# The reciprocal root of a per-row norm: ScalarE's square root against a guess on the bits and three Newton steps on VectorE

## The chip, the cores and the metric

The kernel runs on one core of one Trainium2 chip. The metric is device microseconds of one execution. Five engines work beside each other and meet at semaphores: TensorE (PE; PEld is its weight load), VectorE (DVE), ScalarE (ACT), GpSimd (POOL), which here issues indirect DMAs, and SyncE (SP), which issues plain ones.

## The reference

A graph layer with a GRU cell, then a layer of eight experts, on 6250 rows of 256 values and 200000 edges sorted by their target:

```python
def _layernorm(x, axis=-1, eps=1e-05):
    m = jnp.mean(x, axis=axis, keepdims=True)
    v = jnp.var(x, axis=axis, keepdims=True)
    return (x - m) / jnp.sqrt(v + eps)
...
        msg = h[edge_src] + relvectors[edge_rel]
        red = jax.ops.segment_sum(msg, edge_dst, num_segments=h.shape[0])
        return _gru_cell(red, h, w_ih, w_hh, b_ih, b_hh)
...
        gate_scores = x @ Wg + bg
        _, idx = jax.lax.top_k(gate_scores, K)
...
    x = x + _L0_gnn_ref(_layernorm(x, axis=-1), L0_gnn_relvectors, L0_gnn_w_ih, L0_gnn_w_hh, L0_gnn_b_ih, L0_gnn_b_hh, src, dst, edge_type_16)
    x = x + _L0_ffn_ref(_layernorm(x, axis=-1)[None], L0_ffn_Wg, L0_ffn_bg, L0_ffn_W1, L0_ffn_b1, L0_ffn_W2, L0_ffn_b2)[0]
```

The change concerns the second `_layernorm`, on the rows that the graph layer has left, ahead of the experts.

## The kernel before

The work has four parts. A prologue normalizes `x` (the first norm, in seven chunks, with its own square roots at line 789), writes the result as `h_table` to DRAM and lays out the edges. Then come half steps, numbered h = 0, 1, 2 and on, in which three things run interleaved. (1) The *head*, the first 230 rows of 512 edges: VectorE builds one-hot matrices (`head_build`, tiles `lone`, `cone`, with `wone` and `tone` per pair of rows), PE multiplies them into counts in bursts (`head_burst`, L1704 and L1709), ScalarE copies each burst's counts out of PSUM into `amat` (`move_group`, L827 and L830), and PE multiplies `amat` with the node table in pieces (`head_piece`, L1722). The bursts use two PSUM banks in turn, so a burst waits until the burst ahead of it is copied. (2) The *tail*, the other 162 rows of edges: POOL gathers the source rows by indirect DMAs into `ring` (L709, eight DMAs a step, room for two steps), and PE sums them (`sums`, L1649). While there are bursts in the head, a gather also waits until PE has reached a certain burst (`gather_turns`). (3) The GRU and the choice of experts, tile by tile: 25 tiles of 250 rows, in a fixed order and mostly six half steps apart. When the tiles are done, 56 expert blocks follow (from about 1200 us on).

What each engine does in half step h is written out by hand in four functions `fast` (ScalarE L888, VectorE L1371, PE L1822, POOL L722), with `stage_of(h, n)` naming the tile that is at its stage n. Each engine works through its own list in order, so a wait stops all that is behind it. A tile's stages, with tile i six half steps behind tile i - 1:

- stage 0: PE transposes the rows of the table (`transpose_h`), ScalarE copies them (`copy_hT`, tile `h_h`);
- stage 1: PE multiplies them for the new state (`gate_hn`, L1760), at the end of its half step, when VectorE has `h_l` ready;
- stage 2: VectorE makes the low part of the rows (`low_h`, L1251, tile `h_l`), behind `add_sums`, `build` and `lay_indices`; later `fast_sums`; PE `gate_r`; ScalarE `bias_hn` and the first tanh (`gate_r`, L857);
- stages 3 to 6: the other gates; VectorE blends (`blend`), PE transposes back (`transpose_gru`, L1785), which also waits until the tile ahead has its slots;
- stage 7: VectorE adds the rows of `x` and takes mean and variance (`residual`, L1273), last but one in its half step; ScalarE takes the root (`root`, L872), ahead of that half step's bursts;
- stage 8: VectorE takes the reciprocal and writes the normed rows `xrow` (`second_norm`, L1287); PE transposes them (`transpose_x2`, L1793); POOL later scatters them to `expert_rows`;
- stages 10 to 12: scores, the two best experts (`choose`), their rows' numbers (`number`).

So stage 7 of a tile is stage 1 of the next, and stage 8 of a tile is stage 2 of the next: `residual` of a tile is followed on VectorE by `low_h` of the next one, and PE's `gate_hn` of the next tile waits for that.

ScalarE's square root and its tanh need different tables: the compiler has put a table load (ACT_TABLE_LOAD) ahead of each root and ahead of each tile's first tanh; copies and sums with a bias need none. On VectorE `link` makes every instruction wait until the one ahead has finished.

Of the kernel before, what the change touches and what calls it, by code (L numbers as in the profile page):

```python
# [11 lines left out]
I32 = mybir.dt.int32  # L12
# [3 lines left out]
ALU = mybir.AluOpType  # L16
ACT = mybir.ActivationFunctionType
# [8 lines left out]
EPS = 1e-5  # L26
UP = 2048.0
DOWN = 1.0 / UP
# [37 lines left out]
SUB = 125  # L66
# [167 lines left out]
def groups_of(h):  # L234
    return [g for g in range(len(GROUPED)) if HALF_OF[g] == h]


def bursts_of(h):

    out = []  # L240
    for g in groups_of(h):
        alone = len(BANKS[BANK_OF[g]]) == 1 and GROUPED[g][2] < GC
        before = out[-1][-1] if out else None
        if out and BANK_OF[before] == BANK_OF[g]:
            out[-1].append(g)
        elif out and alone and len(out[-1]) == 1 and len(BANKS[BANK_OF[before]]) == 1 and GROUPED[before][2] < GC:
            out[-1].append(g)
        else:
            out.append([g])
    return out  # L250
# [13 lines left out]
def stage_of(h, offset):  # L264

    return [i for i in range(TILES) if BEGIN[i] + offset == h]
# [51 lines left out]
def gnn_ffn_kernel(nc, x, src, dst, etype, rel, w_ih, w_hh, b_ih, b_hh, Wg, bg, W1, b1, W2, b2,  # L318
# [6 lines left out]
    with ExitStack() as ctx:  # L325
        def sb(name, shape, dt=F32):
            return ctx.enter_context(nc.sbuf_tensor(name, shape, dt))
# [48 lines left out]
        mv = sb("mv", [128, 2, LN_J, 2])  # L376
        var = sb("var", [128, 2, LN_J])
        std = sb("std", [128, 2, LN_J])
        rstd = sb("rstd", [128, 2, LN_J])
        nmr = sb("nmr", [128, 2, LN_J])  # L380
        idx = sb("idx", [128, IDXR, SC], I32)
        onehot = sb("onehot", [128, 2, SC, WIN], F16)
        onetype = sb("onetype", [128, 2, FULL], F16)
# [85 lines left out]
        with ExitStack() as early:  # L469
# [21 lines left out]
            a_ready a_used a_windows a_group a_moved a_cons a_high a_low a_merged a_added s_groups s_slots  # L491
            g_idx g_type g_onehot g_counts g_cts g_agg g_half g_added g_ramp
            h_loaded x_loaded x_stored h_trans hT_ready h_l_ready red_ready hn_done hn_ready r_done r_ready rhn_ready
            z_done z_ready in_done pre_n n_ready gru_ready gru_trans x1_ready var_ready std_ready x2n_ready x2_trans
            x2h_ready x2l_ready scores_done mask_ready ranks_done slots_ready
            raw_loaded w_maxed w_tops w_trans w_diag w_spread w_scales w_high w_low w_stored w_loaded
            head_free tab_ready late_loaded
# [7 lines left out]
         a_ready, a_used, a_windows, a_group, a_moved, a_cons, a_high, a_low, a_merged, a_added, s_groups, s_slots,  # L505
         g_idx, g_type, g_onehot, g_counts, g_cts, g_agg, g_half, g_added, g_ramp,
         h_loaded, x_loaded, x_stored, h_trans, hT_ready, h_l_ready, red_ready, hn_done, hn_ready, r_done, r_ready, rhn_ready,
         z_done, z_ready, in_done, pre_n, n_ready, gru_ready, gru_trans, x1_ready, var_ready, std_ready, x2n_ready, x2_trans,
         x2h_ready, x2l_ready, scores_done, mask_ready, ranks_done, slots_ready,
         raw_loaded, w_maxed, w_tops, w_trans, w_diag, w_spread, w_scales, w_high, w_low, w_stored, w_loaded,  # L510
         head_free, tab_ready, late_loaded,
# [259 lines left out]
        def _(act):  # L771
# [39 lines left out]
            def move_counts(n):  # L811
                act.wait_ge(counts_done, n + 1)
                nc.scalar.activation(cts[:, :], P[0][:, 256:256 + STEP_G * WIN], ACT.Copy).then_inc(cts_ready, 1)
# [19 lines left out]
            def high_sums(b):  # L833
                act.wait_ge(a_cons, b + 1)
                if b:
                    act.wait_ge(a_merged, b)
                used = BATCHED[b][1] * BATCHED[b][2]
                nc.scalar.activation(s_h[0:used, :], P[1 + 3 * (b % 2)][0:used, 0:D], ACT.Copy).then_inc(a_high, 1)

            def copy_hT(i):  # L840
                act.wait_ge(h_trans, i + 1)
                if i:
                    act.wait_ge(gru_ready, i)
                nc.scalar.activation(h_h[:, :, :].rearrange("p k t -> p (k t)"), P[6][:, 0:KT * T], ACT.Copy, scale=DOWN).then_inc(hT_ready, 1)

            def bias_hn(i):
                act.wait_ge(hn_done, i + 1)
                if i:
                    act.wait_ge(gru_trans, i)
                for m in range(KT):  # L850
                    ins = nc.scalar.activation(oT[:, m, :], P[7][:, m * T:(m + 1) * T], ACT.Identity, bias=bhhc[:, 4 + m:5 + m])
                ins.then_inc(hn_ready, 1)
# [16 lines left out]
                    ins = nc.scalar.activation(rT[:, m, :], oT[:, m, :], ACT.Tanh, bias=bihc[:, 4 + m:5 + m])  # L869
                ins.then_inc(n_ready, 1)  # L870

            def root(i):  # L872
                act.wait_ge(var_ready, i + 1)
                nc.scalar.activation(std[0:SUB, 0, 0:2], var[0:SUB, 0, 0:2], ACT.Sqrt, scale=DOWN * DOWN).then_inc(std_ready, 1)

            def high_x2(i):
                act.wait_ge(x2_trans, i + 1)
                nc.scalar.activation(x2h[:, :, :].rearrange("p k t -> p (k t)"), P[5][:, 0:KT * T], ACT.Copy).then_inc(x2h_ready, 1)
# [9 lines left out]
            def fast():  # L888
                act.wait_ge(s_small, 1)
                move_counts(0)  # L890
                for h in range(ENDS):
                    n, s = divmod(h, 2)
                    for i in stage_of(h, 2):
                        bias_hn(i)
                    for i in stage_of(h, 7):
                        root(i)
                    if h + 4 in ADDED_AT:
                        high_sums(ADDED_AT.index(h + 4))
                    bursts = bursts_of(h)
                    for g in bursts[0] if bursts else []:  # L900
                        move_group(g)
                    for i in stage_of(h, 0):
                        copy_hT(i)
                    for i in stage_of(h, 2):
                        gate_r(i)
                        if 1 <= i <= WJOBS:
                            high_weights(i - 1)
                    for i in stage_of(h, 4):
                        gate_z(i)
                        gate_n(i)  # L910
                    for g in groups_of(h)[len(bursts[0]):] if bursts else []:
                        move_group(g)
                    for i in stage_of(h, 8):
                        high_x2(i)
                    if s == 1 and n + 1 < NS:
                        move_counts(n + 1)

            def general():
                act.wait_ge(s_small, 1)
                for b in range(BANDS):  # L920
                    with act.Fori(0, STEPS * BW) as v:
                        act.wait_ge(g_counts, v + (b * (STEPS * BW) + 1))
                        nc.scalar.activation(cts[:, :], P[0][:, 256:256 + STEP_G * WIN], ACT.Copy).then_inc(g_cts, 1)
                    for i in range(b * BT, b * BT + BT):
                        copy_hT(i)
                        bias_hn(i)
                        gate_r(i)
                        if 1 <= i <= WJOBS:
                            high_weights(i - 1)
                        gate_n(i)  # L930
                        gate_z(i)
                        root(i)
                        high_x2(i)

            paths(act, fast, general)

            def high_rows(b):
# [29 lines left out]
        def _(dve):  # L967
            count = [0]

            def link(ins):  # L970
                count[0] += 1
                ins.then_inc(dve_chain, 1)
                dve.wait_ge(dve_chain, count[0])
# [299 lines left out]
            def residual(i):  # L1273
                dve.wait_ge(gru_trans, i + 1)
                dve.wait_ge(x_loaded, 16 * (i + 1))
                x1f = x1[:, :, :].rearrange("p j d -> p (j d)")
                nc.vector.tensor_tensor(x1f, P[5][0:SUB, :], x1f, ALU.add).then_inc(x1_ready, 1)
                dve.wait_ge(x1_ready, i + 1)
                for j in range(2):
                    ins = nc.vector.bn_stats(st[0:SUB, j, :], x1[:, j, :])  # L1280
                link(ins)
                for j in range(2):
                    ins = nc.vector.bn_aggr(mv[0:SUB, 0, j, :], st[0:SUB, j, :])
                link(ins)
                nc.vector.tensor_scalar_add(var[0:SUB, 0, 0:2], mv[0:SUB, 0, 0:2, 1], EPS).then_inc(var_ready, 1)

            def second_norm(i, t):  # L1287
                dve.wait_ge(std_ready, i + 1)
                if i >= 2:
                    dve.wait_ge(scattered[i % 2], 64 * (i // 2))  # L1290
                link(nc.vector.reciprocal(rstd[0:SUB, 0, 0:2], std[0:SUB, 0, 0:2]))
                nc.vector.tensor_scalar(xrow[:, i % 2, :, D:D + 1].bitcast(I32), tok[0:SUB, :].unsqueeze(2), float(T * t), None, ALU.add)
                for j in range(2):
                    ins = nc.vector.tensor_scalar(xrow[:, i % 2, j, 0:D], x1[:, j, :], mv[0:SUB, 0, j, 0:1], rstd[0:SUB, 0, j:j + 1],
                                                  ALU.subtract, ALU.mult)
                ins.then_inc(x2n_ready, 1)
# [691 lines left out]
```

## Time and profile before

| | |
|---|---|
| time before, median of 3 runs | 1543.21 us (1542.58 to 1543.78) |
| profiled execution, own time | 1541.31 us |
| its span | 1539.3 us |
| its mean granted clock of TensorE | 0.922 |
| share of the span: PE, DVE, ACT, POOL | 84%, 65%, 48%, 65% |
| ACT_TABLE_LOAD, ahead of L874 and of L857 | 25 and 25, 32.1 us each |

The profile is of one execution. A row of a timeline names start, duration, engine, line, operation, what is written and read, and in brackets how long the engine stood idle before and what ended that. "issue" is idle time that nothing in the profile explains. A row of the waits names who waited for whom, the sum, the number of times and the longest.

### The profile page before, as it was taken

What the parts mean: (1) busy time and instruction counts of PE and PEld (TensorE: products, weight loads), DVE (VectorE), ACT (ScalarE), POOL (GpSimd) and SP (SyncE); (2) the same over time, 40 slices, a digit from 0 to 9 for tenths busy, and PEclk for the clock granted to TensorE, in tenths of its full rate; (3) what the DMA queues carried; (4) which work ended last, traced back from release to release, by engine and by line L of the source; (5) the groups of instructions that cost most, each with busy time, mean ns of one, the idle gap of its engine ahead of it and who ended that gap; (6) DMA issues with size and microseconds to landing.
All of it is one profiled execution on the core that took longest, in us unless ns stands there. A gap on an engine that the chain in (4) does not pass through costs nothing. (4 is left out here: it accounts for less than half of the span.)

```text
span 1539.3 us, 36184 instructions
## 1 busy us (share of the span) xinstructions
PE 1289.3 (84%) x12887; PEld 1054.1 (68%) x12887; DVE 1002.2 (65%) x2768; ACT 732.5 (48%) x1489; POOL 993.8 (65%) x868
## 2 busy tenths in 40 slices
PE   1159998999999999999998989876464799999995
PEld 1135566777677777777777777765364699999995
DVE  7866765666677777777788877873355455555552
ACT  6524454554444555555444433321122576677663
POOL 2077764776667777777777777777753265555554
PEclk9659999999999999999999989987686899999998
DMA  9586622544445455454544544444762455555551
GB/s 291 177 203 185 192 82 85 144 130 111 117 124 140 140 144 145 138 148 136 137 138 138 143 128 119 112 115 123 246 181 57 101 88 91 97 90 86 91 97 25
DMA packets 131963, 201.46 MB, mean 131 GB/s; under 512 B 28356, under 2 KB 99549, under 8 KB 130631
## 3 DMA queue, kind: packets, MB, share of 16 engines
q0 software_dynamic: 60032, 110.76, 30.0%
q1 hardware_dynamic: 71751, 88.31, 19.8%
q8 instruction: 111, 1.82, 0.5%
q14 instruction: 69, 0.57, 0.1%
HBM read 152.03 MB, written 51.10 MB: 132 GB/s over the span
## 5 line engine op out<-in xcount | busy, mean ns | idle before, releaser
L709 POOL DMA_INDIRECT ring<-h_table,idx x648 | 681.9, 1052 | 293.4 <-issue 210.5
L1722 PE MATMUL P<-hs,amat 128*126 128x512 f16 (+4 forms) x1568 | 404.7, 391 | 0.0
L827 ACT ACTIVATE amat<-P 128x300 f16<-128x300 f32 (+4 forms) x440 | 175.9, 446 | 250.3 <-PE P L1709 249.0
L763 POOL DMA_INDIRECT out_dram<-yo,xrows x112 | 177.3, 1583 | 161.2 <-DVE yo L1586 106.4
L1722 PEld LDWEIGHTS P<-hs,amat 128*126 128x126 f16 (+4 forms) x1568 | 182.4, 130 | 93.3 <-issue 8.6
L1704 PE MATMUL P<-cone,lone 128*128 128x294 f16 (+4 forms) x920 | 181.5, 293 | 44.3 <-ACT amat L827 38.2
L1577 DVE SCALAR_TENSOR_TENSOR gl<-gT,scales,gh 128x512 f16<-128x512 f32 x112 | 84.9, 758 | 138.9 <-ACT gh L954 138.9
L718 POOL DMA_INDIRECT expert_rows<-xrow,slots x100 | 125.2, 1252 | 66.7 <-DVE slots L1329 36.6
L1186 DVE TENSOR_TENSOR cone<-src_t,twice 128x1176 f16<-128x1176 f16 (+4 forms) x230 | 164.4, 715 | 0.0
L1936 PE MATMUL P<-xh,w_all 128*128 128x256 f16 x896 | 157.5, 274 | 0.0
L1949 PE MATMUL P<-w_all,gh 128*128 x896 | 149.8, 273 | 0.6 <-DVE gl L1577 0.6
L1704 PEld LDWEIGHTS P<-cone,lone 128*128 128x128 f16 x920 | 80.2, 100 | 97.9 <-ACT amat L827 48.4
L950 ACT ACTIVATE gT<-P,b1cur,scales 128x256 f32<-128x256 f32 x224 | 113.3, 555 | 43.8 <-PE P L1936 43.8
L830 ACT ACTIVATE amat<-P 128x500 f16<-128x500 f32 (+1 forms) x124 | 81.0, 660 | 101.9 <-PE P L1709 98.7
L1186 DVE TENSOR_TENSOR lone<-slo,twice 128x512 f16<-128x512 f16 x230 | 96.3, 419 | 42.1 <-PE P L1704 41.6
L1936 PE MATMUL P<-xl,w_all 128*128 128x256 f16 x448 | 122.9, 274 | 0.0
L1949 PE MATMUL P<-w_all,gl 128*128 x448 | 122.1, 273 | 0.0
L1649 PE MATMUL P<-onehot,ring 128*128 128x48 f16 x2592 | 87.4, 189 | 37.4 <-DMA ring<-h_table,idx 37.4
L1649 PEld LDWEIGHTS P<-onehot,ring 128*128 128x128 f16 x2592 | 80.5, 100 | 39.0 <-DMA ring<-h_table,idx 39.0
L1756 PE MATMUL P<-h_h,whh_h 128*128 128x250 f32 x300 | 92.8, 309 | 6.3 <-DVE h_l L1251 6.3
L1151 DVE TENSOR_TENSOR acc<-P,acc 128x96 f32 x162 | 41.6, 257 | 82.5 <-PE P L1649 56.0
L1936 PEld LDWEIGHTS P<-xh,w_all 128*128 x896 | 88.2, 98 | 10.3 <-issue 0.2
(244 smaller groups left out, 2734.9 us busy)
## 6 DMA issues: line engine op xcount, KB each, us to landing
raw<-in_L_ffn_W_dram SPq DMA_DIRECT2D x32, 512.0 KB
xrows<-expert_rows SPq DMA_DIRECT2D x56, 257.0 KB, 3.1
ring<-h_table,idx POOLq DMA_INDIRECT x648
w_parts<-parts SPq DMA_DIRECT2D x16, 512.0 KB
w_all<-w_parts SPq DMA_DIRECT2D x8, 1024.0 KB
h_in<-h_table SPq DMA_DIRECT2D x25, 250.0 KB
x<-in_x_dram SPq DMA_DIRECT2D x25, 250.0 KB
out_dram<-x SPq DMA_DIRECT2D x25, 250.0 KB
```

The source lines that it names most:

```text
L709: nc.gpsimd.indirect_dma_start(out=ring[:, r, j, :], out_offset=None, in_=h_dram, in_offset=bass.IndirectOffsetOnAxis(ap=idx[:, slot, g * ...
L718: nc.gpsimd.indirect_dma_start(out=xs_dram, out_offset=bass.IndirectOffsetOnAxis(ap=slots[:, i % 2, c * 2 + j:c * 2 + j + 1], axis=0), in_ ...
L763: nc.gpsimd.indirect_dma_start(out=out, out_offset=bass.IndirectOffsetOnAxis(ap=xrows[:, b % XR, j, D:D + 1].bitcast(I32), axis=0), in_=yo ...
L827: nc.scalar.activation(amat[:, b % 2, :, s * aw:(s + 1) * aw], bank[:, 0:HIS * aw].rearrange("p (h w) -> p h w", w=aw), ACT.Copy).then_inc ...
L950: ins = nc.scalar.activation(gT[:, b % 2, s, :], P[2 + p % 3][:, (s % 2) * TB:(s % 2 + 1) * TB], ACT.Gelu, bias=b1cur[:, b % 2, s:s + 1], ...
L1186: return nc.vector.tensor_tensor(chunk_pairs(buf, row, size), of.unsqueeze(2).to_broadcast(shape), nums.unsqueeze(1).to_broadcast(shape), ...
L1649: ins = nc.tensor.matmul(to, ring[:, r * STEP_G + g, j, at:at + 128], onehot[:, k, g * GC + j, :], start=False, stop=(g == STEP_G - 1 and ...
L1704: nc.tensor.matmul(counts_of(g, aw)[:, 0:HI * aw], src_of[:, m, :, t], dst_of[:, m, :, t], start=(n == 0), stop=(n == k - 1)).then_inc(a_u ...
L1722: nc.tensor.matmul(both, amat[:, b % 2, hi, 0:used], hs[:, hi, :], start=(hi == 0), stop=False)
L1756: ins = nc.tensor.matmul(to, a[:, k, row + m * 128:row + (m + 1) * 128], b[:, k, :], start=(n == 0), stop=(n == len(ops) - 1))
L1936: ins = nc.tensor.matmul(to, weights(b, a * WCH + k * H + s * 128, 128), v[:, b % 2, k, :], start=(n == 0), stop=(n == len(ops) - 1))
L1949: ins = nc.tensor.matmul(to, a[:, b % 2, s, j * 128:(j + 1) * 128], weights(b, (2 + w) * WCH + s * D, D), start=(n == 0), stop=(n == len(o ...
```

## The change

ScalarE's `root`, its two calls and the semaphores `var_ready` and `std_ready` go. In `residual` the variance plus epsilon is also scaled by DOWN squared, where the activation's `scale` did so; then VectorE halves the bits as an integer, subtracts them from a constant (a first guess of the reciprocal root) and improves the guess in three Newton steps of three instructions. Every one of the 12 is linked to the one before. The reciprocal in `second_norm` goes, and with it its wait for the root.

```diff
@@ -378,6 +378,7 @@
         nmr = sb("nmr", [128, 2, LN_J])
+        newton = sb("newton", [128, 4, 2])
         idx = sb("idx", [128, IDXR, SC], I32)
...
@@ -869,10 +870,6 @@
-            def root(i):
-                act.wait_ge(var_ready, i + 1)
-                nc.scalar.activation(std[0:SUB, 0, 0:2], var[0:SUB, 0, 0:2], ACT.Sqrt, scale=DOWN * DOWN).then_inc(std_ready, 1)
-
             def high_x2(i):
...
@@ -892,8 +889,6 @@
                     for i in stage_of(h, 2):
                         bias_hn(i)
-                    for i in stage_of(h, 7):
-                        root(i)
                     if h + 4 in ADDED_AT:
...
@@ -1282,13 +1276,19 @@
                 for j in range(2):
                     ins = nc.vector.bn_aggr(mv[0:SUB, 0, j, :], st[0:SUB, j, :])
                 link(ins)
-                nc.vector.tensor_scalar_add(var[0:SUB, 0, 0:2], mv[0:SUB, 0, 0:2, 1], EPS).then_inc(var_ready, 1)
+                v, y, a, bits = [newton[0:SUB, n, :] for n in range(4)]
+                link(nc.vector.tensor_scalar(v, mv[0:SUB, 0, 0:2, 1], EPS, DOWN * DOWN, ALU.add, ALU.mult))
+                link(nc.vector.tensor_scalar(bits.bitcast(I32), v.bitcast(I32), 1, None, ALU.logical_shift_right))
+                link(nc.vector.tensor_scalar(y.bitcast(I32), bits.bitcast(I32), -1.0, float(0x5F3759DF), ALU.mult, ALU.add))
+                for step in range(3):
+                    link(nc.vector.tensor_tensor(a, y, v, ALU.mult))
+                    link(nc.vector.scalar_tensor_tensor(a, a, -0.5, y, ALU.mult, ALU.mult))
+                    to = y if step < 2 else rstd[0:SUB, 0, 0:2]
+                    link(nc.vector.scalar_tensor_tensor(to, a, 1.5, y, ALU.add, ALU.mult))
 
             def second_norm(i, t):
-                dve.wait_ge(std_ready, i + 1)
                 if i >= 2:
                     dve.wait_ge(scattered[i % 2], 64 * (i // 2))
-                link(nc.vector.reciprocal(rstd[0:SUB, 0, 0:2], std[0:SUB, 0, 0:2]))
                 nc.vector.tensor_scalar(xrow[:, i % 2, :, D:D + 1].bitcast(I32), tok[0:SUB, :].unsqueeze(2), float(T * t), None, ALU.add)
```

The order of instructions on VectorE, at stage 7 of tile 11 of the order (the twelfth) and the beginning of the next half step, up to `h_l` of the next tile. Before:

```order
L1277 TENSOR_TENSOR x<-P,x 125x512
L1280 BN_STATS st<-x 125x6 x2
L1283 BN_AGGR mv<-st 125x2 x2
L1285 TENSOR_SCALAR var<-mv 125x2
L1151 ISA
L1151 TENSOR_TENSOR acc<-P,acc 128x2x48
L1151 ISA
L1151 TENSOR_TENSOR acc<-P,acc 128x2x48
L1129 TENSOR_TENSOR onehot<-dst_t,ramp 128x384
L1132 TENSOR_TENSOR onetype<-typ_t,ramp 128x128
L1125 CAST idx<-src_t 128x8
L1251 SCALAR_TENSOR_TENSOR h_l<-P,h_h 128x500
```

The same place of the changed program, whose lines behind the removed `root` have other numbers; first the sum, the guess and the first Newton step:

```order
L1277 BN_AGGR mv<-st 125x2 x2
L1280 TENSOR_SCALAR newton<-mv 125x2
L1281 TENSOR_SCALAR newton<-newton 125x2
L1282 TENSOR_SCALAR newton<-newton 125x2
L1284 TENSOR_TENSOR newton<-newton 125x2
L1285 SCALAR_TENSOR_TENSOR newton<-newton 125x2
L1287 SCALAR_TENSOR_TENSOR newton<-newton 125x2
```

and, behind the second step, which reads as the first, the third one and what follows it:

```order
L1284 TENSOR_TENSOR newton<-newton 125x2
L1285 SCALAR_TENSOR_TENSOR newton<-newton 125x2
L1287 SCALAR_TENSOR_TENSOR rstd<-newton 125x2
L1145 ISA
L1145 TENSOR_TENSOR acc<-P,acc 128x2x48
L1145 ISA
L1145 TENSOR_TENSOR acc<-P,acc 128x2x48
L1123 TENSOR_TENSOR onehot<-dst_t,ramp 128x384
L1126 TENSOR_TENSOR onetype<-typ_t,ramp 128x128
L1119 CAST idx<-src_t 128x8
L1245 SCALAR_TENSOR_TENSOR h_l<-P,h_h 128x500
```

Where one instruction stood between the aggregates and the sums there are now 12; all that follows, `h_l` among it, keeps its order and moves behind them.

ScalarE at the same place, from the copy of the next tile's `h_h` to the first tanh. Before:

```order
L844 ACTIVATE h_h<-P 128x500
L827 ACTIVATE amat<-P 128x50x5
L830 ACTIVATE amat<-P 128x50x10 x2
L874 ACT_TABLE_LOAD
L874 ACTIVATE std<-var 125x2
L830 ACTIVATE amat<-P 128x50x10 x3
L813 ACTIVATE cts<-P 128x96
L851 ACTIVATE oT<-P,bias 128x250 x2
L830 ACTIVATE amat<-P 128x50x10
L857 ACT_TABLE_LOAD
L857 ACTIVATE rT<-P,half_rz 128x250 x2
```

and now:

```order
L845 ACTIVATE h_h<-P 128x500
L828 ACTIVATE amat<-P 128x50x5
L831 ACTIVATE amat<-P 128x50x10 x5
L814 ACTIVATE cts<-P 128x96
L852 ACTIVATE oT<-P,bias 128x250 x2
L831 ACTIVATE amat<-P 128x50x10
L858 ACTIVATE rT<-P,half_rz 128x250 x2
```

The root and both loads are gone, and the five copies of counts follow each other. In the whole changed program three loads are left: one ahead of the first norm's roots, one ahead of the first tanh and one ahead of the experts' gelu. The order of PE, POOL and SP is the same as before.

## Rows read from the trace of the kernel before

**Rows 1.** The page's engine totals: busy us, share of the span, instructions.
```profile
PE 1289.3 (84%) x12887; PEld 1054.1 (68%) x12887; DVE 1002.2 (65%) x2768; ACT 732.5 (48%) x1489; POOL 993.8 (65%) x868
```

**Rows 2.** POOL's waits, 767 to 1140 us: sum in us, times, longest.
```profile
POOL ring L709 <- issue: 59.1, 194, 0.3
...
POOL ring L709 <- PE P L1709: 7.6, 25, 0.3
POOL ring L709 <- PE P L1649: 2.4, 8, 0.3
```

**Rows 3.** POOL's waits, 200 to 766 us.
```profile
POOL ring L709 <- PE P L1709: 38.5, 50, 3.6
```

**Rows 4.** TensorE's waits, 910 to 1075 us.
```profile
PE P L1649 <- DMA ring<-h_table,idx: 12.7, 4, 4.3
...
PE P L1756 <- DVE h_l L1251: 3.7, 3, 2.3
```

**Rows 5.** ScalarE's waits, whole span.
```profile
ACT rT L857 <- PE P L1756: 37.0, 25, 2.0
```

**Rows 6.** ScalarE's timeline, turn 11: start us, us, instruction, idle before it.
```profile
695.91 1.28 ACT L874 ACT_TABLE_LOAD   x1
698.36 0.20 ACT L874 ACTIVATE std<-var 125x2 f32<-125x2 f32 x1 [1.17 <-DVE var L1285]
```

**Rows 7.** TensorE's timeline, turns 11, 5 and 13.
```profile
699.34 0.39 PE L1704 MATMUL P<-cone,lone 128*128 128x245 f16 x2 [1.21 <-ACT amat L830]
...
700.76 0.47 PE L1756 MATMUL P<-h_h,whh_h 128*128 128x250 f32 x1
...
465.54 0.47 PE L1756 MATMUL P<-h_h,whh_h 128*128 128x250 f32 x1
...
784.13 0.47 PE L1756 MATMUL P<-h_h,whh_h 128*128 128x250 f32 x1
```

**Rows 8.** VectorE's timeline, `low_h` behind turns 11, 5 and 13.
```profile
699.71 0.67 DVE L1251 SCALAR_TENSOR_TENSOR h_l<-P,h_h 128x500 fp32r<-128x500 f32 x1
...
462.77 0.67 DVE L1251 SCALAR_TENSOR_TENSOR h_l<-P,h_h 128x500 fp32r<-128x500 f32 x1
...
782.75 0.67 DVE L1251 SCALAR_TENSOR_TENSOR h_l<-P,h_h 128x500 fp32r<-128x500 f32 x1
```

**Rows 9.** VectorE's timeline, the last turn (24).
```profile
1178.49 0.25 DVE L1283 BATCH_NORM_AGGREGATE mv<-st 125x2 f32<-125x6 f32 x2
1178.77 0.17 DVE L1285 TENSOR_SCALAR var<-mv 125x2 f32<-125x2 f32 x1
1179.21 0.17 DVE L1291 RECIPROCAL rstd<-std 125x2 f32<-125x2 f32 x1 [0.27 <-ACT std L874]
1179.41 0.61 DVE L1292 TENSOR_SCALAR xrow<-cols 125x2 int32<-125x2 f32 x1
```

**Rows 10.** VectorE's timeline, two linked short instructions of `choose`.
```profile
1184.08 0.17 DVE L1306 TENSOR_TENSOR scores<-P,bgb 125x16 f32<-125x16 f32 x1 [1.12 <-PE P L1801]
1184.29 0.17 DVE L1307 TENSOR_TENSOR scores<-P,scores 125x16 f32<-125x16 f32 x1
```

**Rows 11.** POOL's timeline, two gathers at 846 and 847 us.
```profile
845.96 0.96 POOL L709 DMA_INDIRECT ring<-h_table,idx  x1 [0.30 <-DVE idx L1125]
847.22 0.96 POOL L709 DMA_INDIRECT ring<-h_table,idx  x1 [0.30 <-issue]
```

**Rows 12.** TensorE's timeline, the sums that free those gathers' buffers.
```profile
842.88 0.96 PE L1649 MATMUL P<-onehot,ring 128*128 128x48 f16 x32
```

**Rows 13.** TensorE's timeline, the last turns.
```profile
1131.46 0.58 PE L1756 MATMUL P<-h_h,whh_h 128*128 128x250 f32 x1
...
1142.16 0.30 PE L1649 MATMUL P<-onehot,ring 128*128 128x48 f16 x5 [1.97 <-DMA ring<-h_table,idx]
...
1158.51 0.58 PE L1756 MATMUL P<-h_h,whh_h 128*128 128x250 f32 x1 [2.64 <-DVE h_l L1251]
```

**Rows 14.** VectorE's timeline, short comparisons of `choose` at 847 us.
```profile
847.16 0.26 DVE L1317 TENSOR_TENSOR m<-ramp,topf 125x16 f32<-125x16 f32 x2
```

More of the change, by code:

```diff
@@ L493, in gnn_ffn_kernel @@
             h_loaded x_loaded x_stored h_trans hT_ready h_l_ready red_ready hn_done hn_ready r_done r_ready rhn_ready
-            z_done z_ready in_done pre_n n_ready gru_ready gru_trans x1_ready var_ready std_ready x2n_ready x2_trans
+            z_done z_ready in_done pre_n n_ready gru_ready gru_trans x1_ready x2n_ready x2_trans
             x2h_ready x2l_ready scores_done mask_ready ranks_done slots_ready
@@ L507, in gnn_ffn_kernel @@
          h_loaded, x_loaded, x_stored, h_trans, hT_ready, h_l_ready, red_ready, hn_done, hn_ready, r_done, r_ready, rhn_ready,
-         z_done, z_ready, in_done, pre_n, n_ready, gru_ready, gru_trans, x1_ready, var_ready, std_ready, x2n_ready, x2_trans,
+         z_done, z_ready, in_done, pre_n, n_ready, gru_ready, gru_trans, x1_ready, x2n_ready, x2_trans,
          x2h_ready, x2l_ready, scores_done, mask_ready, ranks_done, slots_ready,
@@ L931, in general @@
                         gate_z(i)
-                        root(i)
                         high_x2(i)
```

## The prediction

> **What bounds the kernel now.** I read the page's engine totals first, then the waits by stretch, then single turns in the timeline. A "turn" is a tile of 250 rows in the order of the work, 0 to 24.
>
> The totals [rows 1] show TensorE (PE) busy 84% and GpSimd (POOL) 65%. That share hides that POOL is a full queue for a quarter of the span. From 767 to 1140 us, 194 of its waits before a gather are "issue", and the longest of any kind is 0.3 us, those that PE ended too [rows 2]: it issues one gather behind the other and nobody holds it back. In the stretch before it is the other way round: PE's bursts ended 50 waits of 38.5 us, the longest 3.6 us [rows 3], and the view of PE's own waits has none for a gather there. So up to 765 us PE's order of work sets the time; from 765 to 1140 us the gathers do, and PE waits for them (four waits, 12.7 us, between 910 and 1075 us) [rows 4]; behind 1140 us it is one chain through PE, VectorE (DVE) and ScalarE (ACT) until the last tile is sorted. The expert blocks follow unchanged.
>
> **What the change removes: nearly nothing that anyone waits for.** ScalarE loses 25 roots and 49 of its 52 table loads (the order of the changed program has 3 left). 25 of the loads stand ahead of the first tanh; behind that load ScalarE still waited for PE in all 25 turns, 37.0 us in total [rows 5]. So these are hidden, and that they go is worth nothing. The other 24 go with the roots. In turn 11 the load of 1.28 us runs at 695.91 us, and the root waits for `var` until 698.36 us [rows 6]; copies of the counts stand behind it, and PE stood 1.21 us for them at 699.34 us. But PE's next wait, `gate_hn` of the next tile at 700.76 us [rows 7], is for `h_l` from VectorE, which was done at 700.38 us (699.71 + 0.67) [rows 8]. Getting there earlier is no use if `h_l` gets later. That stall is the longest of the three that lie right behind a root before 765 us; I credit them with **0**.
>
> **What it adds: a chain on VectorE.** The sum of variance and epsilon stays one instruction; 11 follow it in `residual` (2 on the bits, 9 in three steps), on 125x2 numbers, each linked to the one before; the reciprocal in `second_norm` goes. Their rate is shown by linked short instructions: from the reciprocal on 125x2 at 1179.21 us to its successor at 1179.41 us it is 0.20 us [rows 9], and two linked sums start at 1184.08 and 1184.29 us, 0.21 us apart [rows 10]. I take 0.205 us: with one link more `residual` ends 11 x 0.205 and some 0.05, **2.3 us later**. Without the reciprocal, VectorE's work grows by 25 x 2.1 = 52 us. Bounds: 0.17 us, the length of one such instruction, since a linked one can't begin before the one ahead is through, gives 1.9 us; 0.28 us, as from the two aggregates at 1178.49 to `var` at 1178.77 us [rows 9], gives 3.1 us.
>
> The first thing behind the chain that PE needs is `h_l`: `residual` stands at the end of one half step, `low_h` near the start of the next, and PE's `gate_hn` waits for it. The normed row, which the root fed, is needed only by PE's transposes half a step later, with over 2.3 us to spare in nearly every turn. So a turn costs 2.3 us less the time that `h_l` now lies ready before `gate_hn` starts:
>
> - Before 765 us seven of 13 turns have 2.4 us or more and lose nothing. The six others have 2.10 (turn 5: 462.77 + 0.67 against 465.54 us), 1.62, 2.05, 1.89, 1.10 and 0.38 us (turn 11) [rows 7, 8]. Against 2.3 that is 0.2 + 0.7 + 0.3 + 0.4 + 1.2 + 1.9 = **4.7 us**. PE loses them and POOL, paced by PE here, with it.
> - Between 765 and 1140 us the same sum is larger. Turns 13, 15 and 16 have 0.71 (782.75 + 0.67 against 784.13 us) [rows 7, 8], 1.32 and 1.34 us and lose 1.6 + 1.0 + 1.0; in turns 17 to 19 PE already waits for `h_l` (three waits, 3.7 us) [rows 4] and loses 2.3 each: 10.5 us together. But here POOL sets the pace, and PE's waits for gathers, 12.7 us, take the late work up. A gather is held only if PE gets later than its buffer lay free. The tightest I find begins at 845.96 us [rows 11], while the sums that free its buffer ran in the first half of 842.88 to 843.84 us [rows 12]: some 2 us of reserve, when PE would be 1.6 us late. I cost this stretch at **0**; its cover is POOL's backlog, and without that the price is the 10.5 us.
> - Behind 1120 us: the `gate_hn` at 1131.46 us comes 2.3 us later, but PE stood 1.97 us for the last gather at 1142.16 us: **0.3 us** stay. At 1158.51 us PE had waited 2.64 us for `h_l` alone [rows 13]: **2.3 us**. In turn 24 everything waits for the norm: from `var` at 1178.77 to the row's first instruction at 1179.41 us it is 0.64 us now [rows 9]; the chain takes 12 x 0.205 = 2.46 us: **1.8 us**.
>
> **Sum:** 0 + 4.7 + 0 + 0.3 + 2.3 + 1.8 = **+9.1 us**. The profiled execution took 1541.3 us, 1.9 us under the median of the runs; the same difference on the median of 1543.2 us gives 1552.3, so **1552 us**. By the bounds: at 0.17 us the six turns cost 2.6 and the end 3.3 us, +5.9 (1549.1 us); at 0.28 us nine turns cost 11.2 and the end 6.9 us, +18.1 (1561.3 us).
>
> **A rule against the trace.** By the row of turn 11 the 49 loads that go are 49 x 1.28 = 63 us of ScalarE's time, and by the wait rows they are worth nothing. The Trainium skill (ScalarE: Activation LUTs, What ACT_TABLE_LOAD costs) states 1283 ns for the load and some 1380 ns more for a drain at each switch of sets; its rules for kernel authors ask to do all of one set before switching. By that the change would save ScalarE 49 x 2.66 = 130 us (an estimate from that page). The trace agrees on the load's length; that ScalarE's time matters here it does not show.
>
> **The rivals.**
>
> 1. *PE's lost time reaches the end in full.* If POOL's backlog is smaller than I read it, the 10.5 us of the middle are added: 1543.2 + 9.1 + 10.5 = 1562.8 us. For it: the reserve of 2 us at 845.96 us is narrow. Against: POOL's waits of 0.3 us through 373 us.
> 2. *Only the end counts.* If the first stretch's 4.7 us are taken up, because PE, later at `gate_hn`, stands less at its next waits for VectorE, the end's 4.4 us stay: 1547.6 us.
> 3. *Faster: the copies behind the root were the bound.* Without load and root the first copy of counts behind them comes up to 1.28 + 0.20 = 1.49 us earlier [rows 6]. If PE turned that into time in all 13 turns before 765 us it would gain 19.3 us against 9.1 us of costs: 10.2 us faster, 1533 us. It decides from 0.7 us a turn on (9.1 / 13). Against: the longest of three stalls right behind a root is 1.21 us. The rule above speaks for this case.
> 4. *POOL is held by the new instructions.* If each of the 12 held up a gather's issue for its 0.17 us, the nine turns of the stretch that POOL sets (13 to 21) would pay 9 x 2.0 = 18 us more: 1570 us. Against: the gather issued at 847.22 us took 0.96 us [rows 11] beside short comparisons at 847.16 us [rows 14], as long as the one ahead of it. The Trainium skill (SBUF — State Buffer, SBUF: two separate sides) states that VectorE and GpSimd share a pair of ports under an exclusive lock, and that descriptors aren't written while VectorE holds it; that instructions as short as these do it the row does not show.
>
> That the loads might stay is excluded by the order; that the guess on the bits costs more than other instructions of its size is inside the upper bound.
>
> **How the numbers follow.** A measurement of this kernel can tell about 0.2%, 3.1 us, from no change. My forecast gets 0.58, the first rival 0.14, the second 0.10, the third 0.12, the fourth 0.03; 0.03 is left for no effect at all. The range leaves out the third and fourth rival and little else: from 1545 us (the second rival with the short instruction, 3.3 us, is 1546.5; the rest is the runs' own scatter) to 1563 us (the first). Faster: 0.10 (most of the third). The same: 0.10 (no effect, the rest of the third, half of the second). Slower: 0.80.
>
> **What would show it right or wrong.** Right: 12 short instructions a turn at 0.20 to 0.21 us each; 3 table loads; PE waits for `h_l` in a dozen turns; its waits for gathers up to 1075 us shrink by some 10 us; POOL's last wait for PE stays near 765 us, moved by some 5 us; the expert blocks begin 9 us later and take as long as before. Wrong: POOL waiting for PE behind 850 us (rival 1), a first stretch that ends no later (2), fewer waits of PE for ScalarE's copies and a first stretch that ends earlier (3), or gathers that take longer than now (4).

## The result and the profile after

The changed kernel took 1561.64 us (median of 6 runs, 1552.81 to 1567.36), the kernel before 1543.49 us (median of 6) beside it: ratio 1.0106 [1.0073, 1.0139] (in brackets the 95% interval). The medians lie 18 us apart; the ratio makes it 16 us, and 16 is used below. The forecast was 1552 us, range 1545 to 1563. A second comparison gave 1.0104 [1.0083, 1.0125]. The profiled execution of the changed kernel took 1552.81 us, the shortest of its runs. So single profiles are used below for where time goes, and sums come from ratios.

The engine totals, which answer to [rows 1]:

```profile
PE 1287.4 (83%) x12887; PEld 1053.8 (68%) x12887; DVE 1044.1 (67%) x3018; ACT 667.1 (43%) x1415; POOL 1002.0 (65%) x868
```

VectorE has 250 instructions and 42 us more, ScalarE 65 us less: 49 table loads went. Nothing stood still for them: ScalarE's wait behind the first tanh, 37.0 us before [rows 5], is now longer. The waits view (whose columns are the sum in us, the times and the longest):

```profile
ACT rT L858 <- PE P L1756: 70.7, 25, 4.0
```

The new chain, by lines of VectorE (busy us, mean ns of one, idle before):

```profile
L1285 DVE SCALAR_TENSOR_TENSOR newton<-newton 125x2 f32<-125x2 f32 x75 | 12.3, 164 | 2.6
L1284 DVE TENSOR_TENSOR newton<-newton 125x2 f32<-125x2 f32 x75 | 12.2, 163 | 2.6
...
L1280 DVE TENSOR_SCALAR newton<-mv 125x2 f32<-125x2 f32 x25 | 6.7, 267 | 0.9
L1282 DVE TENSOR_SCALAR newton<-newton 125x2 int32<-125x2 int32 x25 | 5.2, 207 | 0.9
L1281 DVE TENSOR_SCALAR newton<-newton 125x2 int32<-125x2 int32 x25 | 5.1, 204 | 0.9
```

The nine instructions with two inputs take 0.164 us and 0.035 us before them (2.6 / 75): 0.20 us each, as forecast. The three with one input take 0.20 to 0.27 us in the mean; why is seen in the last section. TensorE's waits over the whole span:

```profile
PE P L1704 <- ACT amat L828: 36.3, 40, 6.0
...
PE P L1756 <- DVE h_l L1245: 30.9, 13, 6.5
PE P L1649 <- DMA ring<-h_table,idx: 30.8, 11, 7.5
```

The wait for `h_l` had been 3.7 us in three times in the middle [rows 4] and 2.6 us at the end [rows 13]. Now there are 13. The same view from 200 to 766 us, where before no wait for `h_l` was listed:

```profile
PE P L1756 <- DVE h_l L1245: 7.6, 5, 3.1
```

And POOL's waits from 770 to 1144 us, which answer to [rows 2]: it is still a full queue.

```profile
POOL ring L710 <- issue: 64.6, 212, 0.3
...
POOL ring L710 <- PE P L1709: 4.3, 14, 0.3
POOL ring L710 <- PE P L1649: 1.5, 5, 0.3
```

One turn shows the mechanism. VectorE behind turn 10 (start us, us), to be read against [rows 8]; lines left out are the rest of the chain and the work between it and `h_l`:

```profile
656.50 0.25 DVE L1277 BATCH_NORM_AGGREGATE mv<-st 125x2 f32<-125x6 f32 x2
656.78 0.59 DVE L1280 TENSOR_SCALAR newton<-mv 125x2 f32<-125x2 f32 x1
657.40 0.17 DVE L1281 TENSOR_SCALAR newton<-newton 125x2 int32<-125x2 int32 x1
...
659.42 0.16 DVE L1287 SCALAR_TENSOR_TENSOR rstd<-newton 125x2 f32<-125x2 f32 x1
659.72 0.26 DVE L1145 TENSOR_TENSOR acc<-P,acc 128x96 f32 x1
...
661.09 0.67 DVE L1245 SCALAR_TENSOR_TENSOR h_l<-P,h_h 128x500 fp32r<-128x500 f32 x1
```

From the aggregates to `h_l` done it is 5.3 us. TensorE in the same turn, two of the twelve matmuls of `gate_hn`:

```profile
661.82 0.45 PE L1756 MATMUL P<-h_h,whh_h 128*128 128x250 f32 x1 [2.18 <-DVE h_l L1245]
...
662.28 0.42 PE L1756 MATMUL P<-h_h,whh_l 128*128 128x250 f32 x1
662.50 0.41 PE L1756 MATMUL P<-h_h,whh_h 128*128 128x250 f32 x1
```

It stood 2.18 us, and then its matmuls came 0.21 us apart. The same matmuls of the kernel before, which had not waited, came 0.12 us apart:

```profile
662.06 0.28 PE L1756 MATMUL P<-h_h,whh_l 128*128 128x250 f32 x1
662.18 0.28 PE L1756 MATMUL P<-h_h,whh_h 128*128 128x250 f32 x1
```

The windows of the changed kernel around that stall (window, its us, busy us of PE, PEld, DVE, ACT and POOL with counts, granted clock, DMA share, GB/s):

```profile
658.00:661.50 3.50, 1.64 (x12) 1.00 (x9) 2.91 (x14) 0.68 (x1) 2.61 (x3) 1.00 0.96 256
662.00:665.40 3.40, 3.27 (x24) 2.92 (x25) 3.11 (x8) 0.40 (x2) 2.48 (x4) 0.50 0.82 242
666.00:669.00 3.00, 3.00 (x45) 3.00 (x42) 2.79 (x11) 0.54 (x2) 2.39 (x3) 1.00 0.45 123
```

For 3.4 us behind this stall the granted clock is 0.50, that is 1.2 GHz instead of 2.4. By this row the stall cost its length and up to half of such a stretch, 1.7 us (an estimate). Not every stall did: behind the longest one before 765 us, in turn 11, the matmuls came 0.12 us apart again.

```profile
704.54 0.38 PE L1756 MATMUL P<-h_h,whh_h 128*128 128x250 f32 x1 [3.05 <-DVE h_l L1245]
704.76 0.28 PE L1756 MATMUL P<-h_l,whh_h 128*128 128x250 f32 x1
704.88 0.28 PE L1756 MATMUL P<-h_h,whh_l 128*128 128x250 f32 x1
```

### The profile page after: what moved, and what is told of

Same layout as the page of the kernel before. It is cut to its first block and busy times, and to the rows that moved or that the text cites. A ratio compares the mean times of both kernels' runs of the same rounds, so it can differ in the third digit from the quotient of the medians.

```text
span 1551.0 us, 36343 instructions
## 1 busy us (share of the span) xinstructions
PE 1287.4 (83%) x12887; PEld 1053.8 (68%) x12887; DVE 1044.1 (67%) x3018; ACT 667.1 (43%) x1415; POOL 1002.0 (65%) x868
## 5 line engine op out<-in xcount | busy, mean ns | idle before, releaser
L710 POOL DMA_INDIRECT ring<-h_table,idx x648 | 689.5, 1064 | 297.1 <-issue 215.8
L1722 PE MATMUL P<-hs,amat 128*126 128x512 f16 (+4 forms) x1568 | 399.2, 387 | 0.0
L1180 DVE TENSOR_TENSOR lone<-slo,twice 128x512 f16<-128x512 f16 x230 | 96.5, 420 | 40.1 <-PE P L1704 39.5
L1949 PEld LDWEIGHTS P<-w_all,gh 128*128 128x128 f16 x896 | 87.7, 98 | 11.6 <-issue 1.3
```

Of the source, the lines that this page charges most:

```text
L710: nc.gpsimd.indirect_dma_start(out=ring[:, r, j, :], out_offset=None, in_=h_dram, in_offset=bass.IndirectOffsetOnAxis(ap=idx[:, slot, g * ...
L1180: return nc.vector.tensor_tensor(chunk_pairs(buf, row, size), of.unsqueeze(2).to_broadcast(shape), nums.unsqueeze(1).to_broadcast(shape), ...
L1722: nc.tensor.matmul(both, amat[:, b % 2, hi, 0:used], hs[:, hi, :], start=(hi == 0), stop=False)
L1949: ins = nc.tensor.matmul(to, a[:, b % 2, s, j * 128:(j + 1) * 128], weights(b, (2 + w) * WCH + s * D, D), start=(n == 0), stop=(n == len(o ...
```

## The experiments

Diffs are against the changed kernel. The table has what the profiles say by stretch: from TensorE's first transpose of `oT` (L1785 in both kernels) in turn 0 to that in turn 12; from the 417th gather, about where POOL's last longer wait for PE ended, to the 648th and last; from there to the last `slots` of VectorE.

| kernel | ratio to before [95%] | turn 0 to 12, us | gathers, us | end, us |
|---|---|---|---|---|
| before; second profile | 1 | 512.8; 513.7 | 369.2; 372.6 | 53.4; 53.0 |
| changed; second profile | 1.0106 [1.0073, 1.0139]; 1.0104 [1.0083, 1.0125] | 522.4; 522.3 | 376.2; 373.5 | 55.6; 56.0 |
| e1, neither | 0.9987 [0.9973, 1.0000] | 510.4 | 374.0 | 51.7 |
| e2, both | 1.0082 [1.0058, 1.0107] | 523.1 | 377.5 | 54.8 |
| e3, late | 0.9995 [0.9980, 1.0010] | 512.5 | 374.6 | 51.5 |
| e6, turns 0 to 12 | 1.0086 [1.0063, 1.0110] | 524.3 | 372.9 | 51.4 |
| e7, turns 13 to 21; e7b | 1.0025 [1.0008, 1.0042], both | 513.3; 513.4 | 374.1; 376.0 | 54.0; 56.2 |
| e8, turns 22 to 24 | 1.0004 [0.9991, 1.0018] | 512.7 | 373.9 | 55.1 |
| e10, two steps | 1.0052 [1.0034, 1.0070] | 519.4 | 373.1 | 55.2 |
| e5, six steps | 1.0305 [1.0281, 1.0329] | 541.9 | 384.3 | 58.6 |
| e9, two steps, late | 1.0014 [0.9996, 1.0033] | 515.0 | 373.3 | 54.7 |

**A second profile of each.**

> The changed kernel once more, for a second profile. Median ratio to the kernel before 1.007 to 1.014 as in the first comparison. If the longer gathers are the change's doing, the stretch from POOL's last wait for PE to the last gather is again some 376 us (369 in the kernel before), and gathers of more than 2.5 us appear in it; if they were chance of one execution, it is back near 369 us. The same for the two half-clock stretches of TensorE in the turn that followed the 2.2 us stall at 661 us.

> The kernel before once more, for a second profile. The stretch from POOL's last wait for PE to the last gather was 369.2 us in its first profile and 374.0 and 374.5 us in the two kernels that cost nothing. If 369 us was chance of one execution, it is 372 to 376 us now, and the middle cost the changed kernel nothing or nearly; if it is again 369 us, the middle has a cost of some 5 us that even the kernels without late h_l pay. Turn 0 to turn 12 of TensorE: 512 to 513 us by either.

Turn 0 to 12 repeats within 1 us in either kernel. The gathers don't: 369.2 and 372.6 us before, 376.2 and 373.5 us after, 374.0 us in a kernel without any chain. The 7 us that the first pair of profiles shows there is thus largely scatter between executions. In that stretch gathers over 2.5 us appear in both profiles of the changed kernel and in neither of before, but in e1 (2.8 us) and e3 (3.1 us) too, which cost nothing. (The kernel before took 1547.3 us in that one run, median of its others 1542.7 us.) From turn 10 to turn 12 TensorE ran at half clock for some 6.8 us in both profiles of the changed kernel, and in those of before only for the last 0.7 and 1.3 us. But of the two stretches in the changed kernel's first profile one began at 648.3 us, ahead of the stall at 661 us, and e1, e3, e7 and e9, whose `h_l` is not late there, have one of 3.4 us about the beginning of turn 10 too.

**Neither, or both.** e1:

```diff
-                v, y, a, bits = [newton[0:SUB, n, :] for n in range(4)]
...
-                    link(nc.vector.scalar_tensor_tensor(to, a, 1.5, y, ALU.add, ALU.mult))
+                link(nc.vector.tensor_scalar(rstd[0:SUB, 0, 0:2], mv[0:SUB, 0, 0:2, 1], 0.0, 0.75 * UP, ALU.mult, ALU.add))
```

> Neither root nor Newton steps: one instruction writes a constant in place of the second norm's reciprocal root (that root is left out). Theory (the cost is the 11 linked instructions ahead of h_l; the roots and loads on ScalarE were hidden): as the kernel before, 1541 to 1544 us, PE's waits for h_l back to some 6 us, the gather stretch back to 369 us. Rival (the copies behind the root bound the first stretch): some 10 us faster, 1533 us. Rival (it is the going of the roots that costs, because ScalarE's copies now come at other times): as the changed kernel, 1555 us or more.

e2 puts `root` and its waits back and keeps the chain without its `v`, writing to a tile that nothing reads:

```diff
+                nc.vector.tensor_scalar_add(var[0:SUB, 0, 0:2], mv[0:SUB, 0, 0:2, 1], EPS).then_inc(var_ready, 1)
...
-                    to = y if step < 2 else rstd[0:SUB, 0, 0:2]
-                    link(nc.vector.scalar_tensor_tensor(to, a, 1.5, y, ALU.add, ALU.mult))
+                    link(nc.vector.scalar_tensor_tensor(y, a, 1.5, y, ALU.add, ALU.mult))
...
+                link(nc.vector.reciprocal(rstd[0:SUB, 0, 0:2], std[0:SUB, 0, 0:2]))
```

> The root and its table loads stay, and the 11 linked instructions are added in the same place; nothing reads their result. Theory (the roots' going is worth nothing, the linked instructions cost all): as the changed kernel, ratio 1.008 to 1.014, PE waits for h_l some 30 us. Rival (the roots' going gave back part of a larger cost): slower than the changed kernel by what it gave, up to 10 us more. Rival (the roots' going costs): nearer to the kernel before.

Without both it is 2 us faster (0 to 4 us by the interval), not 10: the forecast's third rival falls. With both it is as slow as the changed kernel, within the intervals. So the linked instructions carry the cost, and 49 loads of 1.28 us were worth at most 4 us.

**The chain in another place.**

```diff
                 link(ins)
+
+            def second_norm(i, t):
                 v, y, a, bits = [newton[0:SUB, n, :] for n in range(4)]
...
-
-            def second_norm(i, t):
                 if i >= 2:
```

> The same 12 instructions a turn, but behind low_h and the other work of the next half step, at the head of second_norm, so that h_l no longer waits for them. Theory (the cost comes through h_l being late): PE waits for h_l back to some 6 us, only the last turn's 1.8 us stays, ratio 1.000 to 1.003 (1543 to 1548 us), and the gather stretch back to 369 us. Rival (52 us more of VectorE's work cost wherever they stand, by bunching the wide builds that lie beside the gathers): ratio 1.007 or more and the gather stretch at 374 us or more although h_l is on time.

The same instructions cost nothing there (-0.8 us, -3 to +1.5). VectorE behind turn 10 of that kernel:

```profile
657.56 0.25 DVE L1277 BATCH_NORM_AGGREGATE mv<-st 125x2 f32<-125x6 f32 x2
657.95 0.26 DVE L1145 TENSOR_TENSOR acc<-P,acc 128x96 f32 x1
...
659.33 0.67 DVE L1245 SCALAR_TENSOR_TENSOR h_l<-P,h_h 128x500 fp32r<-128x500 f32 x1
```

2.4 us from the aggregates to `h_l` done, not 5.3. TensorE's waits for it, whole span, against 6.3 us in four times before:

```profile
PE P L1756 <- DVE h_l L1245: 9.5, 4, 3.4
```

This is the experiment that decides: VectorE's new work (42 us of busy time) is free, its place ahead of `low_h` is not. The gather stretch of 374.6 us, which the rival had named, says nothing, since before has 372.6 us in its second profile.

**Which turns pay.** Three kernels have the chain in `residual` for one stretch and late for the others (here e6; e7 has `13 <= i <= 21`, e8 `i >= 22`; the chain stands in `root_by_steps`):

```diff
+                if i <= 12:
+                    root_by_steps()
...
             def second_norm(i, t):
+                if not (i <= 12):
+                    root_by_steps()
```

> The 12 linked instructions stand in residual for turns 0 to 12 and at the head of second_norm for the later ones. As the prediction priced that stretch: +4.7 us on the 1542.2 us of the kernel with all of them late, 1547 us (ratio 1.003). As the profiles of the changed kernel have it (turn 0 to turn 12 takes 522.4 us instead of 512.5): +10 us, 1552 us (1.006). If later stretches took it up: 1543 us.

> They stand in residual for turns 13 to 21 alone. As predicted (POOL's gathers cover it): 1542 us (ratio 1.000), PE's waits for h_l between 767 and 1140 us some 17 us instead of 7. Rival (full pass-through, 10.5 us): 1553 us (1.006). Rival (late and bunched builds of VectorE make the gathers beside them longer): some 3 us, 1545 us, and the sum of POOL's own times in that stretch above 295 us.

> The linked instructions in residual for turns 13 to 21 alone, once more, because 1.0025 [1.0008, 1.0042] lies between the prediction for this stretch (1.000) and the full price (1.006). If the middle costs something, the median is again 1545 to 1549 us; if it was scatter, 1541 to 1544 us.

> They stand in residual for turns 22 to 24 alone. As predicted: +2.6 us on the kernel with all of them late (0.3 for the h_l behind turn 22 and 2.3 behind turn 23; the last turn pays in both), 1545 us (1.001). By the profiles, where the stretch from the last gather to the last slots is 55.6 and 56.0 us in the changed kernel and 51.5 with all late: +4.3 us, 1546.5 us (1.002). Rival (taken up by the waits behind): 1542 us.

Against all late (0.9995) the first stretch costs 0.91%, 14 us (some 10 to 18 by the two intervals; an estimate), above both figures expected; the middle 0.30%, 4.6 us, the same in both comparisons; turns 22 to 24 0.09%, 1.4 us and no different from nothing. The last turn's cost is in none of the three, since all late pays it too. Their sum, 1.30% on 0.9995, is 1.0125; the whole change has 1.0106 [1.0073, 1.0139]. The first stretch carries most of it. Its windows, turn 0 to 12, for before and its second profile, e3, the changed kernel and its second profile, e6 and e9, in this order:

```profile
220.72:733.55 512.83, 475.10 (x4831) 373.51 (x4829) 359.73 (x1063) 259.84 (x550) 367.62 (x343) 0.99 0.46 130
```
```profile
223.19:736.87 513.68, 476.81 (x4833) 374.93 (x4829) 359.29 (x1063) 259.54 (x550) 367.83 (x343) 0.98 0.46 130
```
```profile
219.77:732.24 512.47, 477.19 (x4832) 375.82 (x4829) 377.51 (x1183) 228.28 (x514) 376.09 (x342) 0.98 0.45 130
```
```profile
214.83:737.27 522.44, 478.11 (x4831) 375.97 (x4829) 379.56 (x1183) 228.38 (x514) 370.35 (x343) 0.98 0.45 128
```
```profile
218.94:741.26 522.32, 480.57 (x4831) 377.47 (x4829) 377.93 (x1183) 228.12 (x514) 369.29 (x343) 0.98 0.44 128
```
```profile
220.05:744.33 524.28, 480.94 (x4831) 378.00 (x4829) 378.84 (x1183) 228.30 (x514) 372.54 (x343) 0.97 0.44 128
```
```profile
217.46:732.50 515.04, 480.81 (x4833) 378.45 (x4829) 371.88 (x1147) 228.32 (x514) 374.64 (x341) 0.97 0.46 130
```

The mean of the changed kernel's two and e6 is 523.0 us against 513.0 of the first three: +10.0. TensorE's busy time, for the same matmuls, is 479.9 against 476.4 us: +3.5, with the clock lower. Its waits for `h_l` there are 7.6, 6.2 and 7.3 us, 7.0 in the mean, against none. The two make 10.5 us where 10.0 were measured. That the 3.5 us come of the late `h_l` isn't shown: e9, which doesn't wait for `h_l` there, has 480.8 us of matmul time at the same mean clock as e6, and takes 515.0 us.

In the middle the cover is thin. POOL's waits for PE's sums, 767 to 1137 us, in e3 and then in e7b:

```profile
POOL ring L710 <- PE P L1649: 1.2, 4, 0.3
```
```profile
POOL ring L710 <- PE P L1655: 3.3, 9, 0.9
```

A gather was held 0.9 us in e7b (and in e7), none over 0.3 us in e3, nor in the changed kernel. That is in the direction of the 4.6 us and smaller than it. The rival of longer gathers (1545 us) has the right size, but not its sign: POOL's own times from the 417th gather to the last are 291.5 us in e7 and 294.0 in e7b, not above 295, and 293.2 in e3. What is longer in the two profiles is the end, 54.0 and 56.2 us against 51.5 in e3; but e9, with all late, has 54.7 too. With stretches that scatter by 3 to 5 us between executions, one profile of each doesn't say where the 4.6 us go.

**The length of the chain.** Six steps and two, in place (`range(6)`, `range(2)`):

> Six steps in place of three: 9 more linked instructions, so residual ends another 9 x 0.2 = 1.8 us later in every turn. Theory (every turn whose spare time is used up pays in full): in the changed kernel's profile h_l lies ready less than 0.6 us before PE wants it, or late, in ten of the first thirteen turns, so turn 0 to turn 12 takes some 16 to 18 us more than in the changed kernel (539 us), the end some 5 us; 1582 us, ratio 1.025. If POOL's cover in the middle also breaks, 9 x 1.8 = 16 us more: 1598 us (1.035). Rival (the cost does not grow with the delay): 1560 us (1.010).

> Two steps in place of three, in the same place: residual ends 0.6 us earlier than in the changed kernel. Theory: PE's waits for h_l at the four late turns of the first stretch each shrink by 0.6 us, with half as much again from what goes with them, so turn 0 to turn 12 some 519 us, and 1.2 us less at the end: ratio 1.006 to 1.008 (1553 us). Rival (the cost comes with the chain and does not grow with its length): 1.010.

Both follow the length as forecast: 541.9 (539) and 519.4 us (519) for turn 0 to 12; the ratio with two steps, 1.0052, lies a little under the one expected. Two steps take 6.4 us more than the 513.0 without delay, three 10.0, six 28.9. From three to six, 1.8 us of delay cost 18.9 us: as if ten turns paid all of it. And with six the middle's cover breaks; POOL's wait for PE's sums, 796 to 1180 us:

```profile
POOL ring L710 <- PE P L1649: 11.6, 12, 4.4
```

It has 384.3 us for the gathers. The time, 1590 us, lies between the two expected (1582 and 1598).

**A version for both.** Two steps at the head of `second_norm`:

> Two steps, at the head of second_norm: the shortest chain in the place where it cost nothing; the version that could beat both. Theory: as with three steps there, or up to 1 us less: 1541 to 1543 us, ratio 0.998 to 1.000. Rival (VectorE's time itself counts, 15 us in 25 turns): 3 us or more under the kernel before.

The ratio is 1.0014 [0.9996, 1.0033], the median above the 1541 to 1543 us expected: no better than the kernel before, nor told apart from three steps late. No version here beats the kernel before by more than can be measured.

## Why the prediction was right, and where its sizes were off

The direction and the mechanism were right; the size was 9 us where 16 were measured. That 1561.64 us still lies in the range is in part luck: the range's end at 1563 us was drawn for the first rival, the middle paying 10.5 us in full. The middle paid some 4, and the time came near that end because the first stretch cost two to three times its 4.7 us.

- **The chain's rate**: right, 0.20 us an instruction. In the last turn the aggregates to `rstd` took 2.4 us as worked out, and the wait for the normed row grew by 1.5 us (1.8 forecast):

```profile
1192.50 0.89 PE L1793 MATMUL P<-ident,xrow 125*128 125x125 f32 x3 [5.11 <-DVE xrow L1294]
```

- **Roots and loads at 0**: right for the changed kernel (e1, e2). With `h_l` on time one wait behind a root does count: e3's turn 11 takes 40.4 us against 41.5 before, where TensorE stood 1.21 us for the copies [rows 7]. The Trainium skill (ScalarE: Activation LUTs, What ACT_TABLE_LOAD costs) prices such switches; here the loads were 1283 ns each as it says, and by e1 and e2 what ScalarE saved reached no end. The drain of some 1380 ns that it adds isn't seen: in turn 3 of the kernel before the load begins 0.01 us behind the copy (374.84 + 0.42), and the root 0.01 us behind the load:

```profile
374.84 0.42 ACT L827 ACTIVATE amat<-P 128x300 f16<-128x300 f32 x1
375.27 1.28 ACT L874 ACT_TABLE_LOAD   x1
376.56 0.20 ACT L874 ACTIVATE std<-var 125x2 f32<-125x2 f32 x1
```

- **First stretch at +4.7 us: the step that failed by size.** It is 10 us in the profiles and 14 in the timed comparison. The turns were the right ones: waits at turn 6 (0.7 forecast, 1.52 in the changed kernel's profile), 9 (0.4; 0.64), 10 (1.2; 2.18) and 11 (1.9; 3.05), none at 5 and 8. Turn 10 is off most: from its first transpose to that of turn 11 it takes 45.3 and 43.1 us in the changed kernel's two profiles, against 40.1 us in both of before. The first profile of each (columns as in the windows above):

```profile
648.45:693.77 45.32, 41.05 (x398) 33.09 (x398) 31.82 (x102) 18.27 (x34) 32.18 (x30) 0.93 0.46 128
```
```profile
651.87:692.01 40.14, 37.98 (x397) 30.53 (x398) 29.70 (x92) 20.92 (x37) 30.89 (x30) 1.00 0.54 145
```

  Two things were not in the sum. Behind turns 6, 9 and 10 a one-input instruction of the chain met a scatter of POOL and took 0.61, 0.61 and 0.59 us instead of 0.17, so `residual` ended some 0.4 us later than by the 2.3 (in turn 11 one took 0.46 us, but there `var` had taken 0.47 us before). And matmuls were taken at one duration; part of them ran at half the clock: 3.5 us more matmul time in the mean of the profiles above, and in this pair 3.0 us, all of it in turn 10. That the stalls cause these half-speed stretches is read from their place and not shown: of the two stalls over 2 us in turns 10 and 11 of the changed kernel's first profile one is followed by such a stretch, and e3 has 1.4 us more matmul time than before in turn 10 without a stall. The wait of turn 11 is longer than what it cost: the 1.21 us that TensorE stood there for ScalarE's copies [rows 7] are gone, and it stands for `h_l` instead; the turn is 2.0 us longer in that profile (43.5 against 41.5 us).
- **Middle at 0**: too low; 3.9 us against before, 4.6 against e3. "POOL sets the pace" holds (no full pass-through of 10.5 us, which lies above e7's interval, so the first rival falls). But the late work was not taken up as the prediction says: TensorE's waits for gathers from 910 us on, 12.7 us [rows 4], were to shrink by some 10 us and are still 9.1 us, while it now stands up to 6.5 us for `h_l` at one tile there.

```profile
PE P L1649 <- DMA ring<-h_table,idx: 9.1, 3, 4.5
```

  With six steps the cover breaks. Which gathers, or what else, carry the 3.9 us stays open.
- **End at +4.4 us**: neither borne out nor refuted. The profiles show 2 to 3 us (55.6 and 56.0 against 53.4 and 53.0), less than e3 and e9, both with all late, differ there (51.5 and 54.7). Turns 22 to 24 without the last turn's norm, 2.6 us of the forecast, came to 1.4 us, with an interval of some 3 us either way. The wait behind turn 23 grew as forecast, from 2.64 us [rows 13] by 2.3:

```profile
1168.50 0.58 PE L1756 MATMUL P<-h_h,whh_h 128*128 128x250 f32 x1 [4.97 <-DVE h_l L1245]
```

  But behind the late gate of turn 22 TensorE no longer waited for the last gathers, which had cost it 1.97 us [rows 13], and other waits of the end differ by a microsecond or two between executions.
- **Rivals**: the second (only the end counts) falls by e6 and e8. The third, which needed fewer waits of TensorE for ScalarE's copies, falls by e1. The fourth, that the new instructions hold POOL, has no support: e3, with the same instructions, costs nothing, and POOL's own times from the 417th gather to the last are 294.8 and 292.1 us in the changed kernel, 291.7 in e1, which has no chain, and 287.8 and 290.3 before: not 18 us more. The holds that were seen went the other way.

## What to carry to other kernels

Before moving small work from one engine to another, ask what stands behind it in the new queue, not how busy that engine is: 12 instructions of 0.2 us were free behind `low_h` and cost 16 us ahead of it. Price each turn by the spare time of its first waiting consumer, and allow for slower matmuls: here some of TensorE's stalls were followed by half the clock and others were not. A wait that grows is not the price: part of turn 11's had been a wait for another engine. Where a transfer queue is the cover, count the lateness that already stands in it.

## What was not expected of the hardware

Short VectorE instructions with one input tensor (the sum and the two on the bits) were sometimes held until an indirect DMA of POOL, mostly a scatter, was through, while those with two inputs never were. Behind turn 10 of the changed kernel the scatter ran to 657.40 us, and the sum that began at 656.78 us ended at 657.37 us:

```profile
656.21 1.19 POOL L719 DMA_INDIRECT expert_rows<-xrow,slots  x1 [0.30 <-PE P L1709]
```

In that profile 13 of 75 one-input instructions of the chain took over 0.3 us (up to 0.61) and none of 225 two-input ones (up to 0.23). The eight over 0.4 us all ended 0.02 to 0.03 us before such a scatter's end. With the chain late it is 3 of 75, and 0 of 225. The Trainium skill (SBUF — State Buffer, SBUF: two separate sides) says that VectorE and GpSimd take a shared port pair as an exclusive lock, VectorE for operations in a two-port mode, or with two inputs where GpSimd's operation reads SBUF. The trace agrees with a lock in that VectorE waited here until GpSimd was through, the reverse of the fourth rival. Of the page's second case it gives no example (0 of 225), and which mode or ports these instructions used no run shows.
